# Six slots of the last batch turn their main probabilities on TensorE instead of on POOL and the DMA transpose

## The reference

```
x = x + xattn(layernorm(x), ctx, ctx, mask)            # x (8, 512, 256), ctx (8, 1024, 256)
    q, k, v = query @ w_q, key @ w_k, value @ w_v      # 16 heads of 64
    scores = where(mask, -inf, q k^T / 8);  out = softmax(scores) v;  return out @ w_o
x = x + ffn(layernorm(x))
    y = x @ int4(kernel) + bias + (x @ a) @ b
```

## Time and profile before

| what | value |
|---|---|
| three runs | 498.34, 499.07, 499.17 us; median 499.07 |
| the profiled execution's own time | 497.66 us |
| its span, first to last instruction | 494.3 us |
| mean granted clock of TensorE | 0.984 |
| busy: PE, DVE, POOL, ACT | 446.5 (90%), 405.5 (82%), 398.9 (81%), 326.9 us (66%) |

### The profile page before, as it was taken

The page is one execution under the profiler, slowest core; times in us unless marked ns, Lnnn a source line. Parts: engine busy times, 40 slices in busy tenths (PEclk is TensorE's granted clock), DMA queues, the critical chain, the costliest instruction groups (busy, mean ns, idle before and its releaser), DMA issues.

```text
span 494.3 us, 15468 instructions
## 1 busy us (share of the span) xinstructions
PE 446.5 (90%) x5855; PEld 324.4 (66%) x5855; DVE 405.5 (82%) x1110; ACT 326.9 (66%) x845; POOL 398.9 (81%) x659
## 2 busy tenths in 40 slices
PE   2769989899999999999999999999999999888884
PEld 1335646787766866787666866687667866566672
DVE  4987689888988889887988989798988888877762
ACT  4968657866677666776577766775667666655621
POOL 5687778999798878788788978798797977889941
PEclk9899999999999999999999999999999999999897
DMA  8602996698977995879758996799686876769961
GB/s 291 210 23 53 139 195 108 127 195 170 149 138 152 187 132 110 146 165 174 142 117 144 187 164 116 145 170 169 135 141 122 158 155 128 142 117 176 165 122 37
DMA packets 218817, 71.91 MB, mean 145 GB/s; under 512 B 202785, under 2 KB 216882, under 8 KB 218738
## 3 DMA queue, kind: packets, MB, share of 16 engines
q1 hardware_dynamic: 217680, 69.25, 74.4%
q0 software_dynamic: 480, 1.31, 0.9%
q10 hardware_dynamic: 578, 0.30, 0.2%
HBM read 14.71 MB, written 4.19 MB: 38 GB/s over the span
## 4 chain that ended last, share of the span: by engine, by line
PE 42%; DVE 30%; ACT 14%; POOL 8%; issue 4%; DMA 1%; DVEq 0%; POOLq 0%; ACTq 0%
PE ps_b L921 32%; ACT arena L684 8%; DVE ps_a L810 7%; PE ps_a L989 6%; DVE arena L803 4%; ACT arena L663 2%; DVE arena L792 2%; DVE arena L871 2%; POOL arena L589 2%; PE ps_b L1041 2%; DVE arena L758 2%; POOL arena L593 2%; ACT arena L675 2%; PE ps_b L1010 1%; DVE arena L814 1%
## 5 line engine op out<-in xcount | busy, mean ns | idle before, releaser
L921 PE MATMUL ps_b<-arena 128*128 128x65 f16 (+3 forms) x3324 | 319.2, 248 | 8.7 <-DVE arena L871 5.3
L921 PEld LDWEIGHTS ps_b<-arena 128*128 128x128 f16 x3324 | 220.2, 98 | 83.9 <-issue 7.5
L684 ACT ACTIVATE arena<-ps_a,arena 128x160 f32<-128x160 f32 x512 | 159.6, 396 | 92.2 <-DVE arena L814 82.5
L593 POOL TENSOR_TENSOR arena<-arena 128x512 f16<-128x512 f32 x128 | 148.5, 1160 | 0.0
L589 POOL CAST arena<-arena 128x512 f16<-128x512 f32 x128 | 78.2, 611 | 50.6 <-ACT arena L684 48.5
L810 DVE TENSOR_REDUCE ps_a<-ps_a 128x4 f32<-128x640 f32 x128 | 105.3, 822 | 0.0
L989 PE MATMUL ps_a<-arena 64*128 64x160 f16 x1536 | 75.4, 231 | 12.9 <-ACT arena L684 12.9
L989 PEld LDWEIGHTS ps_a<-arena 64*128 64x128 f16 x1536 | 50.3, 94 | 37.8 <-issue 20.7
L1010 PE MATMUL ps_b<-arena 128*128 128x65 f16 x512 | 71.5, 193 | 0.0
L871 DVE TENSOR_TENSOR arena<-ps_b,arena 128x256 f32<-128x256 f32 x128 | 54.3, 424 | 4.4
L701 ACT ACTIVATE arena<-ps_b 128x512 f16<-128x512 f32 x64 | 38.5, 602 | 27.5 <-PE ps_b L1041 27.5
(11 more groups left out here) (142 smaller groups left out, 424.6 us busy)
## 6 DMA issues: line engine op xcount, KB each, us to landing
arena<-in_x_dram SPq DMA_DIRECT2D x8, 512.0 KB, 6.2
mask_u<-in_x_dram SPq DMA_DIRECT2D x32, 128.0 KB, 3.0
out_dram<-mask_u SPq DMA_DIRECT2D x32, 128.0 KB, 2.7
arena<-arena SPq DMA_TRANSPOSE x128, 4.0
arena<-arena SPq DMA_DIRECT2D x24, 65.0 KB, 2.6
arena<-in_L_xattn_w_q_dram SPq DMA_DIRECT2D x1, 1024.0 KB, 8.6
arena<-in_L_xattn_w_k_dram SPq DMA_DIRECT2D x1, 1024.0 KB, 10.6
arena<-in_L_xattn_w_v_dram SPq DMA_DIRECT2D x1, 1024.0 KB, 12.2
```

The source lines that it names most:

```text
L593: nc.gpsimd.tensor_tensor(lo_main, main, hi_main, ALU.subtract)
L684: ins = nc.scalar.activation(probs[k % 2][:, h, :], p_scores[k % 2][:, h % 2, h // 2 * WINDOW:(h // 2 + 1) * WINDOW], ACT.Exp, bias=neg_ma ...
L921: mm = nc.tensor.matmul(dst, a, c, start=(first and at == 0), stop=(last and at == n - 1))
```

## The change

A set `ON_PE` holds six slots: those of the last batch with k % 4 = 0 (112, 116, 120, 124), and the last two (126, 127). They get one more item, "p", at the end of their late items:

- PE makes four fp32 transposes of the main probabilities into a bank (waiting for the exponentials of k).
- ACT copies the bank as the high half into `pT[k % 4][:, 0]`, DVE subtracts into `pT[k % 4][:, 1]` one slot later.
- POOL leaves out the main part's two instructions in these slots and does only the rest's two.
- The DMA transpose turns only the rest's third in these slots.
- PV of these slots waits for the item p besides the DMA.

The counting of POOL's semaphore for the main high half is adapted, and a new semaphore counts the rest's. The other 122 slots run as before.

```diff
-        SPLIT = ("o0", "o1", "n")
+        SPLIT = ("o0", "o1", "n", "p")
+        ON_PE = {k for k in range(LAST - NS, LAST) if k % NG == 0 or k >= LAST - 2}
...
             late = [(name, k // NG - back) for name, back in LATE[k % NG] if 0 <= k // NG - back < NT]
+            if k in ON_PE:
+                late.append(("p", k))
...
-                sp.dma_start_transpose(
-                    pT[k % TURN_BUFS].rearrange("p i h q -> p (i h) q"),
-                    p_half[k % HALF_BUFS].rearrange("p i h q -> p (i h q)")).then_inc(turned[k % TURN_BUFS], 16)
+                if k in ON_PE:
+                    sp.dma_start_transpose(
+                        pT[k % TURN_BUFS][:, 2],
+                        p_half[k % HALF_BUFS][:, 2].rearrange("p h q -> p (h q)")).then_inc(turned[k % TURN_BUFS], 16)
+                else:
...
-                nc.gpsimd.tensor_copy(hi_main, main).then_inc(p_hi_made, 1)
+                if k not in ON_PE:
+                    nc.gpsimd.tensor_copy(hi_main, main).then_inc(p_hi_made, 1)
...
-                pool.wait_ge(p_hi_made, 2 * k + 1)
-                nc.gpsimd.tensor_tensor(lo_main, main, hi_main, ALU.subtract)
-                pool.wait_ge(p_hi_made, 2 * k + 2)
+                if k not in ON_PE:
+                    pool.wait_ge(p_hi_made, mains_split(k))
+                    nc.gpsimd.tensor_tensor(lo_main, main, hi_main, ALU.subtract)
+                pool.wait_ge(rest_hi_made, k + 1)
...
+                if name == "p":
+                    ins = nc.scalar.activation(pT[s.k % TURN_BUFS][:, 0].rearrange("p h q -> p (h q)"), bank[:, :],
+                                               ACT.Copy)
...
+                if name == "p":
+                    turn = pT[s.k % TURN_BUFS]
+                    nc.vector.tensor_tensor(turn[:, 1].rearrange("p h q -> p (h q)"), bank[:, :],
+                                            turn[:, 0].rearrange("p h q -> p (h q)"), ALU.subtract) \
+                        .then_inc(item_done, 1)
...
                 pe.wait_ge(turned[k % TURN_BUFS], 16 * (k // TURN_BUFS + 1))
+                if k in ON_PE:
+                    pe.wait_ge(item_done, probs_item(k))
...
+                if name == "p":
+
+                    pe.wait_ge(exp_made, s.k + 1)
+                    for e in range(GROUP):
+                        mm = nc.tensor.transpose(bank[:, e * P:(e + 1) * P], probs[s.k % 2][:, e, 0:P], ident[:, :])
```

More of the change, by code:

```diff
@@ L309, in xattn_ffn @@
         p_hi_made = sem("p_hi_made")
+        rest_hi_made = sem("rest_hi_made")
         p_lo_made = sem("p_lo_made")
@@ L435, in end_item, with probs_item, mains_split @@
             return items_at[k] + END_LATE[k].index((name, tile)) + 1
+        def probs_item(k):
+            proj, late = slot_items(k)
+            return items_at[k] + len(proj) + late.index(("p", k)) + 1
+        def mains_split(k):
+            return k + 1 - sum(other <= k for other in ON_PE)
         class Start:
@@ L511, in turn_probs @@
                     sp.wait_ge(pv_made, k - TURN_BUFS + 1)
-                sp.dma_start_transpose(
-                    pT[k % TURN_BUFS].rearrange("p i h q -> p (i h) q"),
-                    p_half[k % HALF_BUFS].rearrange("p i h q -> p (i h q)")).then_inc(turned[k % TURN_BUFS], 16)
+                if k in ON_PE:
[3 more added lines that the diff above has]
+                else:
+                    sp.dma_start_transpose(
+                        pT[k % TURN_BUFS].rearrange("p i h q -> p (i h) q"),
+                        p_half[k % HALF_BUFS].rearrange("p i h q -> p (i h q)")).then_inc(turned[k % TURN_BUFS], 16)
             def rest_values(batch):
@@ L588, in split_probs @@
                 rests = rest_parts(k % HALF_BUFS)
-                nc.gpsimd.tensor_copy(hi_main, main).then_inc(p_hi_made, 1)
+                if k not in ON_PE:
+                    nc.gpsimd.tensor_copy(hi_main, main).then_inc(p_hi_made, 1)
                 nc.gpsimd.tensor_copy(rests[:, :, 0:2, :], rest.unsqueeze(2).broadcast_to([P, GROUP, 2, REST])) \
-                    .then_inc(p_hi_made, 1)
-                pool.wait_ge(p_hi_made, 2 * k + 1)
-                nc.gpsimd.tensor_tensor(lo_main, main, hi_main, ALU.subtract)
-                pool.wait_ge(p_hi_made, 2 * k + 2)
+                    .then_inc(rest_hi_made, 1)
+                if k not in ON_PE:
+                    pool.wait_ge(p_hi_made, mains_split(k))
+                    nc.gpsimd.tensor_tensor(lo_main, main, hi_main, ALU.subtract)
+                pool.wait_ge(rest_hi_made, k + 1)
                 nc.gpsimd.tensor_tensor(rests[:, :, 2, :], rest, rests[:, :, 0, :], ALU.subtract).then_inc(p_lo_made, 1)
@@ L696, in tail_item @@
                 bank = p_item[s.bank(i)]
-                if name == "n":
+                if name == "p":
+                    ins = nc.scalar.activation(pT[s.k % TURN_BUFS][:, 0].rearrange("p h q -> p (h q)"), bank[:, :],
+                                               ACT.Copy)
+                elif name == "n":
                     ins = nc.scalar.activation(x2T_hi.rearrange("p t q -> p (t q)"), bank[:, 0:D], ACT.Copy)
@@ L835, in tail_item @@
                     dve.wait_ge(item_made, s.item(i, 1))
-                if name[0] == "o":
+                if name == "p":
[3 more added lines that the diff above has]
+                        .then_inc(item_done, 1)
+                elif name[0] == "o":
                     m = slice(HT // 2 * int(name[1]), HT // 2 * (int(name[1]) + 1))
```

## The result

| | before | changed kernel |
|---|---|---|
| median of 11 runs each | 498.74 us (496.51 to 500.42) | 492.92 us (491.81 to 497.14) |
| profiled execution: its own time, its span | 497.66, 494.3 us | 492.92, 491.0 us |
| of that outside the span | 3.36 us | 1.9 us |
| mean granted clock | 0.984 | 0.987 |

The ratio, an estimate over all these runs with its 95% interval, is 0.9907 [0.9888, 0.9925] (the two medians alone give 0.988): faster, and by more than forecast. 492.92 lies under the range's low end of 494.5 us. The mean clocks are nearly equal because they take in the whole execution: in its first 50 us the changed kernel's profiled execution has 0.93 where before had 0.97.

The account below looks back on a forecast made before the run. POOL looked like the bound of the last batch, with a DVE, ACT and PE ring only 0.21 us shorter in one round. Terms -0.84 - 3.22 + 1.0 = -3.06 us took 499.07 to 496.0 us, range 494.5 to 499.5.

Parts of the forecast that it names:

- The ring of 10.72 us: Last batch, each round of four slots: a chain through DVE, ACT and PE, only 0.21 us shorter than POOL's round.
- Both low stretches: Half-speed clock after PE's waits before scores(115) and scores(127): both taken as gone, 1.63 + 1.59 us.
- POOL's 0.84 us: Last batch's rounds: POOL stops deciding, gaining 0.21 + 0.63 us and no more, as the ring is next.
- the clock's 3.22: Last batch: added transposes shorten PE's waits, so the clock stays up, 3.22 us; rival that transposes don't hold it, chance 0.16.
- the third round's 0.63 us: exps(125) on ACT, due at 462.90, comes at 463.53 behind POOL; counted as part of POOL's gain.
- The last two slots cost 1.0 us: Slots 126 and 127: two subtractions ahead of normalise(125), for which PV(126) waits, two times 0.6 less a pause.
- DMA ... I count nothing: Six transposes carry a third and land well before PV, three slots later, some 8 us: no gain or loss counted.
- span 494.3, and 3.36 around it: The profiled execution's own 497.66 us, the base against which the change was reckoned part by part.
- the 1.41 us: Profiled execution lies 1.41 us under the median of the runs; carried over to 499.07 us, since no row explains it.
- -3.06: Sum of the change's terms in us: -0.84 for POOL, -3.22 for the clock, +1.0 for the last two slots.

Follow-up runs that it names:

- The fill: Kernel before plus four fp32 transposes that nobody reads on TensorE in slots 112, 116, 120 and 124, POOL as before: 494.31 us, ratio 0.9933.
- fp16 matmuls: Kernel before plus eight fp16 matmuls of 128 columns in slots 112, 116, 120 and 124, POOL as before: 494.69 us, ratio 0.9946.
- POOL's relief: By itself: kernel before without POOL's two main-probability instructions in slots 112, 116, 120 and 124, nothing added on TensorE, ACT or DVE: 499.31 us, ratio 1.002.
- four slots: Changed kernel without slots 126 and 127, which go through POOL and the DMA transpose as before: 491.64 us, ratio 0.9891; again 491.83 us.
- The padding: Kernel before plus never-executed instructions: 16 matmuls in TensorE's program, 497.56 us; or 8 memsets in DVE's program, 496.15 us.

## Why the prediction was wrong

The direction, the two causes inside the span and their sum were right; how the gain divides between the two was not, and the time lies below the range.

- *The ring of 10.72 us behind a full POOL:* right, 10.70 and 10.71.
- *Both low stretches go:* right, 1.67 us in the first and, with POOL's part, 2.23 in the second. The fill shows that the transposes do it. The rule of the Trainium skill, "TensorE: Matmul & The Clock Gate", Part 4 (PE-mode transpose), that transposes don't count the same way, is not borne out here: transposes and fp16 matmuls held 1.00 alike.
- *POOL's 0.84 us and the clock's 3.22:* right as a sum, 4.06, since both were reckoned down to the same ring of 10.72 us; neither holds alone. The clock alone gave 2.2 us, since POOL then decides two rounds and delays the end; POOL's relief on top of it gave 1.93, and by itself nothing (499.31 us). The sum priced POOL by what it held up while the clock was low. Nor is all of the third round's 0.63 us POOL's work. These are the last subtractions of slots 119 and 123, before:

```profile
451.66 0.43 POOL L595 TENSOR_TENSOR arena<-arena 128x128 f16<-128x128 f32 x1
...
462.71 0.43 POOL L595 TENSOR_TENSOR arena<-arena 128x128 f16<-128x128 f32 x1
```

  ACT's exponentials behind them start at 452.18 and 463.53, 0.09 us and 0.39 us after their ends at 452.09 and 463.14. What fills the longer one stays open.
- *The last two slots cost 1.0 us:* 0.87 on the place.
- *"DMA ... I count nothing":* PV indeed did not wait for a transpose in the changed kernel, but I had missed POOL's own wait for them. It was off the ring in the changed kernel (0.44 us), on it with four slots (1.11), and took up POOL's relief where nothing else was changed (1.22).
- *The step that failed is the base of the sum: "span 494.3, and 3.36 around it", carried over as if the change could not touch it.* The 3.36 fell to 1.9 us, with one instruction load less behind the span. The padding shows that the length of DVE's program can do just that, with the span left as it is; in the changed kernel itself it is the likeliest cause. That is 1.4 us of the 3.1 by which the forecast was too high. The other part is the 1.41 us "carried over": the three runs shown had a median of 499.07 us, and larger sets of before 497.4 to 498.7, while the changed kernel's profiled execution is its median run. The last 0.2 us are the span's, -3.3 for -3.06. The profiled pair alone gives 492.92 - 497.66 = -4.74 us, and that is -3.3 and -1.4.

## What to carry to other kernels

A full engine is worth what the next ring leaves: lay the second-longest chain beside it before you credit its relief. Two terms on the same ring can be right together and wrong one by one: here the clock alone gave 2.2 us and POOL's relief alone nothing, and both together some 4.1. So do not price one by a row that the other has shaped. Work that fills an idle TensorE can pay by its clock, here even when nobody reads its result. Compare time less span between two kernels before you explain a difference by its instructions.

## What the hardware showed that was not expected

Eight instructions that are never executed, in DVE's program, took 1.5 us off the time outside the span (3.3 and 1.83 us), with one instruction load less behind the last instruction. TensorE's sixteen took nothing (3.30 us). So an edit that only lengthens one engine's program moved the time of this kernel by 0.2% (ratio 0.9978 [0.996, 0.9997]), at no place that the span shows.
